# Loading the expert weights of the first feed-forward part in its first round, by SP and POOL, and not during the first attention

## What is computed

```python
x = x + _L0_xattn_ref(_layernorm(x), ctx_1024, mask_BxSxS2_ik0, L0_xattn_W, L0_xattn_b)
x = x + _L0_ffn_ref(_layernorm(x), L0_ffn_routers, L0_ffn_W1, L0_ffn_W2)

def _L0_xattn_ref(query, memories, mask, W, b):
    q = jnp.einsum('bsd,od->bso', query, W) + b
    add_mask = (1.0 - mask.astype(q.dtype)) * NEG
    attn_logits = jnp.einsum('bqd,bkd->bqk', q, memories) + add_mask
    attn_weights = jax.nn.softmax(attn_logits, axis=-1)
    return jnp.einsum('bqk,bkd->bqd', attn_weights, memories)

# the first feed-forward part: four rounds, each with its own router, all with the same 16 experts
logits = xt @ router                  # 1600 tokens, 16 experts
probs = jax.nn.softmax(logits)
w, idx = jnp.max(probs), jnp.argmax(probs)
out = w * (jax.nn.silu(xt @ W1[idx]) @ W2[idx])     # W1: 16 x 128 x 512, W2: 16 x 512 x 128
```

## Time and profile before

| What | Before |
|---|---|
| median of 3 runs | 2600.63 us (2598.19 to 2602.44) |
| profiled execution, its own time | 2595.36 us |
| its span, first to last instruction | 2593.7 us |
| mean granted TensorE clock | 0.914 |
| PE busy | 2189.8 us, 84% |
| ACT busy | 1455.0 us, 56% |
| DVE busy | 1301.6 us, 50% |
| POOL busy | 246.2 us, 9% |
| DMA, mean over the span | 352.74 MB, 136 GB/s |

### The profile page before, as it was taken

The page is one execution under the profiler, slowest core; times in us unless marked ns, Lnnn a source line. Parts: engine busy times, 40 slices in busy tenths (PEclk is TensorE's granted clock), DMA queues, the critical chain, the costliest instruction groups (busy, mean ns, idle before and its releaser), DMA issues. The chain is left out here.

```text
span 2593.7 us, 45975 instructions
## 1 busy us (share of the span) xinstructions
PE 2189.8 (84%) x18128; PEld 1478.5 (57%) x18128; DVE 1301.6 (50%) x1692; ACT 1455.0 (56%) x1758; POOL 246.2 (9%) x319
## 2 busy tenths in 40 slices
PE   4777788988889479999748999979966999985998
PEld 2444665846658245666435666646754656654887
DVE  4444334243342566666567777744136666644111
ACT  2225355463454458888537888853235888872342
POOL 1112123141231300000010000010010000000000
PEclk8997998989989689999869999979977999995999
DMA  6884446364463567777046777610034777720000
GB/s 188 254 238 152 146 162 215 113 225 147 162 215 113 157 152 180 180 180 180 15 105 157 180 179 181 162 60 1 0 77 107 180 179 179 180 63 14 17 25 21
DMA packets 118679, 352.74 MB, mean 136 GB/s; under 512 B 20122, under 2 KB 54800, under 8 KB 117872
## 3 DMA queue, kind: packets, MB, share of 16 engines
q1 hardware_dynamic: 103424, 318.21, 45.2%
q0 software_dynamic: 15056, 31.74, 4.3%
HBM read 257.58 MB, written 91.23 MB: 134 GB/s over the span
## 5 line engine op out<-in xcount | busy, mean ns | idle before, releaser
L946 ACT ACTIVATE a_probs<-a_score 128x1200 f32<-128x1200 f32 x768 | 859.2, 1172 | 236.8 <-PE a_score L861 236.8
L861 PE MATMUL a_score<-a_qstack,a_kstack 128*128 128x400 f32 x2304 | 578.8, 373 | 57.1 <-DVE a_qstack L1029 55.7
L861 PEld LDWEIGHTS a_score<-a_qstack,a_kstack 128*128 128x128 f32 x2304 | 379.6, 190 | 229.0 <-issue 168.2
L824 PE MATMUL a_numer<-a_probs,a_v 128*18 128x200 f32 (+1 forms) x9216 | 502.7, 336 | 0.6 <-ACT a_probs L946 0.6
L824 PEld LDWEIGHTS a_numer<-a_probs,a_v 128*18 128x18 f32 (+1 forms) x9216 | 213.3, 97 | 212.4 <-issue 112.8
L1020 DVE TENSOR_TENSOR a_kstack<-a_kraw,a_kstack 64x2888 fp32r<-64x2888 f32 x90 | 284.8, 3164 | 2.9
L1029 DVE TENSOR_TENSOR a_qstack<-a_qrep,k_groupmask 128x1600 fp32r<-128x1600 f32 x48 | 87.6, 1825 | 189.6 <-PE a_score L861 160.7
L1015 DVE CAST a_kstack<-a_kraw 128x2888 fp32r<-128x2888 f32 x90 | 149.5, 1661 | 9.7 <-DVE a_own L1080 9.1
L1486 ACT ACTIVATE f3d_hidden<-f3d_ph,f_b 128x400 f32<-128x400 f32 x128 | 76.1, 594 | 116.0 <-PE f3d_ph L1444 108.7
L1736 ACT ACTIVATE f0r_hidden<-f0r_ph 128x512 f32<-128x512 f32 x112 | 66.9, 597 | 124.6 <-PE f0r_ph L1661 124.6
L1661 PEld LDWEIGHTS f0r_ph<-f0r_xsT,f0r_w 128*128 128x128 f32 x896 | 116.4, 192 | 29.6 <-DVE f0r_xsT L1826 4.2
(11 more groups left out here) (362 smaller groups left out, 2798.3 us busy)
## 6 DMA issues: line engine op xcount, KB each, us to landing
a_kraw<-keys SPq DMA_DIRECT2D x384, 361.0 KB, 6.3
values<-kv_vst SPq DMA_DIRECT2D x32, 1296.0 KB, 5.0
a_v<-values SPq DMA_DIRECT2D x48, 864.0 KB, 4.4
keys<-kv_made SPq DMA_DIRECT2D x48, 722.0 KB, 4.9
l0a_ctxT<-in_ctxT SPq DMA_DIRECT2D x16, 722.0 KB, 9.1
kv_ctxT<-in_ctxT SPq DMA_DIRECT2D x16, 722.0 KB, 8.5
l0a_ctx<-in_ctx SPq DMA_DIRECT2D x16, 704.0 KB
l0a_mask<-in_mask_BxSxS_ik SPq DMA_DIRECT2D x16, 564.1 KB
```

The lines of the kernel that those rows point to most:

```text
L824: last = pe.matmul(numer[32 * g:32 * g + PC, p * 2 * SQ:(p + 1) * 2 * SQ], v[0:rows(t), j, t, (2 * g + p) * PC:(2 * g + p + 1) * PC], prob ...
L861: last = pe.matmul(to, kstack[:, j, g * SK + t * 128:g * SK + (t + 1) * 128], qstack[:, j, g * GH:(g + 1) * GH, :], start=True, stop=not s ...
L946: act.activation(probs[:, n % NP, :].rearrange("p (g q) -> p g q", g=SPAN), slot_ps[:, n % 2, :, 0:GQ], ACT.Exp, scale=HSCALE).then_inc(ex ...
```

## The change

The loop of 32 loads on POOL leaves the first attention. In layer 0's round SP issues the 16 loads of W1 as its first work, counted on a new semaphore up_in, and POOL issues the 16 loads of W2 as its first work, counted on weights_in. PE waits for W2 alone, DVE for W1 alone, at the places where both waited for all 32 before. (The semaphore pooled goes too; it had no reader.)

```diff
@@ l0_attention, POOL @@
-            with pool.Fori(0, E0) as e:
-                pool.wait_ge(scored, e + 1)
-                pool.sem_inc(pooled, 1)
-                pool.dma_start(m.w1[:, bass.ds(e, 1), :].rearrange("p e f -> p (e f)"), ins["L0_W1"][e]).then_inc(m.weights_in, 16)
-                pool.dma_start(m.w2[:, bass.ds(e, 1), :, :].rearrange("p e c d -> p (e c) d"),
-                               ins["L0_W2"][e].rearrange("(c p) d -> p c d", p=128)).then_inc(m.weights_in, 16)
@@ l0_round @@
         @block.sync
         def _(sp):
+            if layer == 0:
+                for e in range(E0):
+                    sp.dma_start(m.w1[:, e, :], ins["L0_W1"][e]).then_inc(m.up_in, 16)
             for pair in (early, late):
...
         @block.gpsimd
         def _(pool):
+            if layer == 0:
+                for e in range(E0):
+                    pool.dma_start(m.w2[:, e, :, :], ins["L0_W2"][e].rearrange("(c p) d -> p c d", p=128)).then_inc(m.weights_in, 16)
             pool.wait_ge(slot_ready, 1)
...
@@ PE @@
-                pe.wait_ge(m.weights_in, 32 * E0)
+                pe.wait_ge(m.weights_in, 16 * E0)
@@ DVE @@
-                dve.wait_ge(m.weights_in, 32 * E0)
+                dve.wait_ge(m.up_in, 16 * E0)
```

More of the change, by code:

```diff
@@ L259, in l0_attention @@
         mask_in = c.sems("mask_in0 mask_in1")
-        m_made, pooled = c.sems("m_made pooled")
+        m_made = c.sem("m_made")
         q1_ready, scored, masked, maxed, exped, turned, kept, outed, added, step = c.sems(
@@ L1869, in __init__ @@
         self.outputs = nc.dram_tensor("outputs", (BLOCKS * 128, D), F32, kind="Internal").ap()
-        self.weights_in, self.router_in, self.cleared = o.sems("weights_in router_in cleared")
+        self.weights_in, self.up_in, self.router_in, self.cleared = o.sems("weights_in up_in router_in cleared")
 def l3_ffn(nc, k, ins):
```

## The result

The changed kernel takes 2588.59 us (median of 7 runs, 2582.86 to 2593.3) against 2600.12 us of the kernel before on the same chip (7 runs): a ratio of 0.995 over all runs (the two medians alone give 0.9956), 95% interval 0.9935 to 0.9965, so 9 to 17 us faster. On another chip it gave 0.9961 (0.9944 to 0.9978, experiment 4). Its profiled span is 2581.3 us against 2593.7 us.

The account below looks back on a forecast made before the run. Transfers were taken to hold the first attention's batches at 10.19 us over a 9.02 us chain. Attention -22 us and first round +6 us gave -16 us: 2585 us from a median of 2600.63 us, range 2577 to 2597.

Parts of the forecast that it names:

- attention, first load: First attention: the ctxT that batch 1's scores wait for comes 1.8 us earlier without one pair of weight loads.
- 13 batches: First attention, batches 2 to 15: 132.52 us falls to 13 x 9.02 us, 15.3 us less; bounds 7 and 15.3 us.
- tail, from the scores of batch 15 on: End of the first attention: an earlier last mask saves 2.6 us of waiting and 1.0 + 1.6 us of half clock, 5 us.
- ACT held for written values: First round: the first write of values queues behind W1, holding ACT's copy of the second batch 12.5 us; bounds 10.5 and 19.
- first block of round 0: First round: 12.5 us hold plus 2.5 us for PE's slow clock minus 9.0 us spare, +6 us; bounds 1.5 and 15.
- round 0 in all: First round: +6 us from SP's queue, with POOL's queue, the two moved waits and later work put at +0.
- The chain of 9.02 us: First attention: PE, ACT and DVE alone need 9.02 us a batch, from an alternating pair of 18.04 us.
- estimate of 8.1 us a batch without weights: First attention: masks of 100 partitions load ten engines, which need 8.1 us a batch without weights and 10.1 us with them.
- DVE's spare of 9.0 us: First round: DVE was through 9.0 us before its first xsT, time that was to hide most of ACT's hold.
- The rival of the full DMA engines: First round: W2 shares the engines and delays xs, 19 us; 2597.6 us, chance 0.07, or 2608.6 us with half the attention's gain, 0.04.
- The rival of the free round: First round: idle DMA and ACT's gaps absorb the loads, only +1.5 us remains; 2580.1 us, chance 0.18.
- The queues' shares: DMA: an engine takes queues in turn, a packet each, so W2 in POOL's queue runs no slower than W1 in SP's.

Follow-up runs that it names:

- experiment 4: Follow-up group on another chip: the changed kernel again without edits, beside two variants that load W1 at the attention's end; the changed kernel gave ratio 0.9961.
- e12: The changed kernel itself, unedited, run again on another chip; ratio 0.9961 to the kernel before, round 0 175.9 us.
- e6: Against the changed kernel, W1's loads stay in POOL's loop of the attention and only W2 is loaded in the round; ratio 0.9939 to the kernel before.
- e7: Against the changed kernel, W2's loads stay in POOL's loop of the attention and only W1 is loaded in the round; ratio 0.9951 to the kernel before.
- e2: Against the changed kernel, SP issues W1 behind the first two writes of values and DVE waits for it behind its early keys; ratio 0.9953.
- e4: Against the changed kernel, both sets load at the attention's end: W1 behind SP's last load, W2 on POOL after batch 14's scores; ratio 0.9974.
- e8: Against the changed kernel, SP issues W1 behind the attention's last load, W2 stays in the round; ratio 0.992 to the kernel before.
- e3: Against the changed kernel, both sets of weights are issued in the layernorm ahead of the round, behind its own loads; ratio 1.0009 to the kernel before.
- e9: Against the changed kernel, W1 behind the attention's last load, eight W2 loads at the attention's end and eight in the layernorm; ratio 0.9956.
- e1: Against the changed kernel, no weight loads; POOL fills W1 and W2 with 0.01 during the attention; ratio 0.9968 to the kernel before.

## Why the prediction was right

2585 us was forecast, 2588.59 us measured, inside the range of 2577 to 2597; faster was given 0.82. Against the median of before, the forecast ratio is 0.994, inside the measured interval. Step by step, from the two profiles:

| Step | Forecast | Measured |
|---|---|---|
| attention, first load | -1.8 us | -2.3 us (scores of batch 2 at 50.84) |
| 13 batches | -15.3 us | 117.04 - 132.52 = -15.5 us |
| tail, from the scores of batch 15 on | -5 us | 14.8 us to the layernorm instead of 20.2: -5.4 us |
| ACT held for written values | 12.5 us | 15.66 us |
| first block of round 0 | +6 us | +8.6 us |
| round 0 in all | +6 us | +9.6 us; +12.8 us in e12 |
| span | -16 us | -12.4 us |

The -12.4 us are -22.7 us at the start of round 0 (attention -23.1 us, and a layernorm 0.4 us longer), +9.6 us in it, +3.2 us in rounds 1 to 3 and -2.5 us behind them. The last two were forecast as nothing and nearly cancel; round 1 alone scatters by more.

**Attention.** The chain of 9.02 us read out of the trace before, one even and one odd batch without a wait, was what the batches then took: 9.00 us. The rule of the Trainium skill that a transfer of 100 partitions runs on ten engines (DMA: Bandwidth & Descriptors, section Why a DMA increments its semaphore by 16 and not by 1), weighed there, gave an estimate of 8.1 us a batch without weights; the chain covers it, so these batches don't test it. With half of the weights still in the loop the same estimate is the middle of 8.1 and 10.1 us, 9.1, where e6's batches take 9.21 us and e7's, with the same bytes in the loop, 9.00 us; it is too near the chain's 9.02 us for either to decide.

**Round.** The mechanism came as written: ACT's wait at the values, PE's fall to 0.50, no DMA wait of the first transposes of xs. The term that was too small is the hold. The weights moved at 316 to 320 GB/s when both queues were full, not 330, and less in the first 5 us (217 GB/s); they were in 27.4 us after the round's start, not 26. The first written values let ACT go 33.0 us into the round, 5.6 us behind the weights' end, where 4.3 us had been counted. 15.66 instead of 12.5 us is 3.2 us, and 2.6 us of it are in the block's start: 15.66 + 2.5 - 9.0 = 9.2 us by my own sum, 8.6 measured. The last +1.0 us (3.1 in e12, block +9.7) lies behind the block's start, where I had put nothing.

**What I had wrong in the reasons.** I took the hold of ACT as the cause and the order in SP's queue as its handle. e2 removed the hold (4.0 us left) and the round did not shorten: what I called DVE's spare of 9.0 us was used up by xs and the keys' writes instead. The rival of the full DMA engines described the bound better, though its price of 19 us was twice what came. By the prediction's own sum e2's round, with a hold of 4.0 us, would have cost nothing, and it cost 9.8 us. So that the sum came near for the changed kernel is luck in part. The rival of the free round (+1.5 us) holds for one set of weights (e7, +0.7 us), not for two.

**The queues' shares.** The rule of the Trainium skill (DMA: Bandwidth & Descriptors, section Queues, rings and completion order), a packet of each queue in turn, held: 877 packets against 875 in the changed kernel's round and 460 against 462 in e4. By it W2 was to be no slower than W1, and W2 was in 2 us ahead of W1 (222.5 and 224.7 us). For e8's first write of values it isn't seen: SP's queue moved nothing beside W2 for 3.7 us after the issue, and whether the write was ready to move by then no trace tells. What it costs the other queue was not weighed: the smaller packets of SP's queue get the smaller part of the bytes, 1.59 of 4.46 MB in the round and 0.24 of 1.74 MB in e4.

## What to carry to other kernels

A load that is moved out of a busy stage pays for itself only up to the free transfer time of the stage it goes to: count the bytes against the idle DMA time there, at the rate of the queue that moves them, and ask whose packets they stand beside. Here 4 MB cost 0.7 to 6 us and 8 MB 10 to 13 us in a stage whose DMA engines had been idle for 13 us. Half of the bytes in each of two gaps (e8) was better than all in one. A gap also closes with its stage: here three stages' ends came late, each 1.6 to 2.0 us behind the last packet of POOL's queue.

## What the runs showed of the hardware

- The time in which SP issued 16 loads of 256 KB depended on what else was moving: 7.6 us (e8), 12.79 us (changed kernel, beside POOL's), 16.2 us (e4) and 20.43 us (e3, behind two contexts). What stands behind them on SP waits.
- A stage's end can stand still for transfers that no instruction in it waits for: in e9 every engine was idle from 185 to 188 us with x complete and all loads issued, in e3 from 209 to 215 us. In both, and at the end of e9's layernorm, the next stage began 1.6 to 2.0 us behind the last packet of POOL's queue. SP's queue was still full when e3's layernorm and e4's attention ended. That POOL's queue is the condition fits all of them and is not tested by an edit.
- With loads waiting in both queues, each moved the same number of packets (877 and 875 in 14 us, 460 and 462 in 6 us), whatever their size.
- Loads of both weights together moved 316 to 320 GB/s at a share of 1.03; W1 alone in SP's queue 387 GB/s at 1.05, W2 alone in POOL's 287 GB/s at 1.02 (e8); with writes of values behind the last of W1 391 GB/s.
- While two fills of 128 x 8192 numbers ran on POOL, 6.94 us each, two instructions of DVE took 12.98 and 12.37 us instead of 0.20 and 0.91 us (e1).
